# Writing row sums element-interleaved in four groups in a four-layer graph kernel

## What is computed

```
def _layernorm(x, axis=-1, eps=1e-05):
    m = jnp.mean(x, axis=axis, keepdims=True)
    v = jnp.var(x, axis=axis, keepdims=True)
    return (x - m) / jnp.sqrt(v + eps)
...
x = _layernorm(x + _L0_gnn_ref(...))   # attention over edges, softmax per target
x = _layernorm(x + _L1_gnn_ref(...))   # mean of neighbours, two linear maps, relu
x = _layernorm(x + _L2_gnn_ref(...))   # one matrix per edge type (8), sum per target
x = _layernorm(x + _L3_gnn_ref(...))   # relu messages of 3 types, 3 node types, residual
```

## Time and profile before

| | us |
|---|---|
| median of 3 runs | 1827.29 (1821.63 to 1827.8) |
| profiled execution | 1824.94 |
| its span on the core | 1822.8 |
| VectorE busy | 1518.1 (83%) |
| TensorE matmul busy | 1447.3 (79%) |
| ScalarE busy | 1085.2 (60%) |
| GpSimd busy | 1221.6 (67%) |

### The profile page before, as it was taken

One profiled execution on the slowest core, in us unless ns is written; L12 is line 12 of the kernel. 1 busy time (PEld: TensorE's weight loads), 2 busy tenths in 40 slices (PEclk: granted clock), 3 DMA queues, 4 the chain that ended last, 5 costly groups with the idle time before them and its releaser, 6 DMA issues.

```text
span 1822.8 us, 24302 instructions
## 1 busy us (share of the span) xinstructions
PE 1447.3 (79%) x6228; PEld 920.3 (50%) x6228; DVE 1518.1 (83%) x4392; ACT 1085.2 (60%) x2688; POOL 1221.6 (67%) x910
## 2 busy tenths in 40 slices
PE   2677777777787737877888499999898499999995
PEld 1344444444454425666666355555555255555552
DVE  3999999999999947999999589999999366666663
ACT  0467777777777754999999735655555233333331
POOL 7467666666766737888883188877772557777764
PEclk8789989899989878999999789999999799999998
DMA  5334444444444335676675445455442333443320
GB/s 145 84 79 100 100 105 105 93 101 97 96 107 105 62 94 126 180 189 181 187 189 159 126 111 128 124 132 138 130 107 76 100 88 88 98 98 90 88 75 21
DMA packets 165804, 205.15 MB, mean 113 GB/s; under 512 B 66823, under 2 KB 97918, under 8 KB 165666
## 3 DMA queue, kind: packets, MB, share of 16 engines
q1 hardware_dynamic: 108066, 179.45, 37.3%
q0 software_dynamic: 57600, 24.15, 7.5%
HBM read 147.12 MB, written 70.80 MB: 120 GB/s over the span
## 4 chain that ended last, share of the span: by engine, by line
DVE 59%; PE 27%; issue 8%; ACT 3%; DMA 1%; SPq 1%; POOL 0%; DVEq 0%; POOLq 0%; ACTq 0%
PE po L1210 16%; DVE bst L660 16%; DVE masked L866 5%; DVE run L738 5%; DVE po L707 4%; DVE sel L709 4%; DVE y L703 3%; DVE po L706 3%; DVE y L698 2%; PE pt L1195 2%; PE po L1205 2%; PE pb L1433 2%; PE pa L1474 1%; PE pc L1474 1%; PE pb L1474 1%
## 5 line engine op out<-in xcount | busy, mean ns | idle before, releaser
L475 POOL DMA_INDIRECT xs<-target_rows,slot_all x276 | 385.7, 1397 | 235.4 <-DMA xs<-source_rows 156.1
L951 ACT ACTIVATE x<-y,nmr,rst 125x128 f32<-125x128 f32 x800 | 322.7, 481 | 47.5 <-DVE nmr L688 47.5
L1210 PE MATMUL po<-wnt,rt 128*125 128x384 f32 x800 | 311.6, 538 | 0.6 <-ACT rt L988 0.6
L475 POOL DMA_INDIRECT xs<-in_x,src_all x100 | 148.1, 1481 | 136.2 <-issue 136.2
L1210 PEld LDWEIGHTS po<-wnt,rt 128*125 128x125 f32 x800 | 172.9, 216 | 117.0 <-issue 40.2
L1205 PE MATMUL po<-ball,ones_bf 128*125 128x512 bf16 (+1 forms) x512 | 153.2, 429 | 80.5 <-DVE sel L709 76.5
L1195 PE MATMUL pt<-ident,x 125*128 125x125 f32 x800 | 125.1, 280 | 99.5 <-issue 73.1
L1210 PE MATMUL po<-wnt,run 128*125 128x384 f32 x600 | 201.5, 486 | 0.0
L482 POOL DMA_INDIRECT out_rows<-do,last_all x100 | 121.5, 1215 | 89.9 <-ACT do L951 48.4
L660 DVE BATCH_NORM_STATS2 bst<-y 125x6 f32<-125x128 f32 x800 | 164.8, 278 | 3.8
L951 ACT ACTIVATE do<-yd,nmr,rst 125x128 f32<-125x128 f32 x400 | 163.6, 482 | 6.6 <-DVE nmr L688 6.6
(11 more groups left out here) (188 smaller groups left out, 3150.0 us busy)
## 6 DMA issues: line engine op xcount, KB each, us to landing
xin<-in_x SPq DMA_DIRECT2D x100, 224.0 KB
out_rows<-res SPq DMA_DIRECT2D x100, 224.0 KB
same<-same_d SPq DMA_DIRECT2D x75, 250.0 KB, 4.0
source_rows<-so SPq DMA_DIRECT2D x75, 224.0 KB
target_rows<-do SPq DMA_DIRECT2D x75, 224.0 KB
xs<-source_rows SPq DMA_DIRECT2D x69, 224.0 KB
xd<-target_rows SPq DMA_DIRECT2D x59, 224.0 KB
rel<-in_etype SPq DMA_DIRECT2D x50, 250.0 KB, 4.7
```

The lines of the kernel that those rows point to most:

```text
L475: return nc.gpsimd.indirect_dma_start(out=to, out_offset=None, in_=table, in_offset=bass.IndirectOffsetOnAxis(ap=index, axis=0), bounds_ch ...
L951: last = A(to[:, j, :], y[:, j, :], ACT.Identity, scale=rst[s][:, k:k + 1], bias=nmr[s][:, k:k + 1])
L1210: last = mm(po[0:R, j * 512:j * 512 + NT * D], left(j), wnt[:, k, :, :].rearrange("k t d -> k (t d)"), start=False, stop=stop, skip_group_ ...
```

## The change

Every tile of sums that goes to `stats` and `normalize` keeps its 512 places per partition, but element d of row group j is written at place d·4 + j instead of j·128 + d. The new view `woven` does that: its step from one element of a row to the next is four float32, that is 16 bytes.

`stats` then issues one `bn_stats` for two groups j and j + 1. Its input runs over d with the pair inside: 256 elements, two neighbours and then a gap of two. The even places are group j and the odd ones group j + 1, so the six numbers are already the two groups' count, mean and sum of squares, and `bst` shrinks to three numbers for each group. `variances` becomes one `scalar_tensor_tensor` and one `tensor_tensor`, with constants from a small tile `floors`; `scales` takes the mean from `bst`. In layer 0 the product of `yd` goes to a plain scratch tile (`ys[0]`) and only the final sum is written woven. The copy of statistics in layer 1 becomes a `tensor_tensor` max of the values with themselves, 12 elements in place of 24. `normalize` reads its 128 values at the 16-byte step and writes them contiguously as before.

```diff
-        bst = two(sb, "bst", [R, G * T, 6])
-        msum, mdif, ve, seed, rst, nmr, tmp = (two(sb, n, [R, G * T]) for n in ...
+        bst = two(sb, "bst", [R, G * T, 3])
+        floors = sb("floors", [R, 2])
...
+        woven = lambda a: a[:, :, :].rearrange("p j d -> p (j d)").rearrange("p (d j) -> p j d", j=T)
...
             def stats(y, s, g):
-                for j in range(T):
-                    last = V.bn_stats(bst[s][:, g * T + j, :], y[:, j, :])
+                for j in range(0, T, 2):
+                    to = bst[s][:, g * T + j:g * T + j + 2, :].rearrange("p j k -> p (j k)")
+                    last = V.bn_stats(to, woven(y)[:, j:j + 2, :].rearrange("p j d -> p d j"))
                 return last
...
-                V.tensor_tensor(md[:, g], b_[:, g, 1], b_[:, g, 4], ALU.subtract)
-                V.tensor_tensor(ms[:, g], b_[:, g, 1], b_[:, g, 4], ALU.add)
-                step(V.tensor_tensor(v[:, g], b_[:, g, 2], b_[:, g, 5], ALU.add))
-                step(V.scalar_tensor_tensor(out=q[:, g], in0=md[:, g], scalar=D / 4.0, in1=md[:, g], ...))
-                step(V.tensor_tensor(v[:, g], v[:, g], q[:, g], ALU.add))
+                v, m2 = ve[s], bst[s][:, :, 2]
                 if twice:
-                    last = V.tensor_scalar(v[:, 0:both], v[:, 0:both], 1.0 + EPS, D * EPS * EPS, ALU.mult, ALU.add)
+                    last = V.scalar_tensor_tensor(out=v[:, 0:both], in0=m2[:, 0:both], scalar=1.0 + EPS,
+                                                  in1=floors[:, 0:1].broadcast_to([R, both]), op0=ALU.mult, op1=ALU.add)
                 if n > twice:
-                    last = V.tensor_scalar(v[:, both:n * T], v[:, both:n * T], D * EPS, None, ALU.add)
+                    last = V.tensor_tensor(v[:, both:n * T], m2[:, both:n * T],
+                                           floors[:, 1:2].broadcast_to([R, n * T - both]), ALU.add)
...
-                    V.tensor_tensor(y0[d % 4][:, :, :], xin[d % 4][:, :, :], bias_rows, ALU.add).then_inc(s_y0, 1)
+                    V.tensor_tensor(woven(y0[d % 4]), xin[d % 4][:, :, :], bias_rows, ALU.add).then_inc(s_y0, 1)
...
-                V.tensor_tensor(yd[b][:, :, :], yd[b][:, :, :], xd3[c % 3][:, :, :], ALU.add).then_inc(q["nF"], 1)
+                V.tensor_tensor(woven(yd[b]), ys[0][:, :, :], xd3[c % 3][:, :, :], ALU.add).then_inc(q["nF"], 1)
...
-                return V.tensor_copy(bst[s][:, T:2 * T, :], bst[s][:, 4 * T:5 * T, :])
+                edge = bst[s][:, 4 * T:5 * T, :]
+                return V.tensor_tensor(bst[s][:, T:2 * T, :], edge, edge, ALU.max)
...
-                    last = A(to[:, j, :], y[:, j, :], ACT.Identity, scale=rst[s][:, k:k + 1], bias=nmr[s][:, k:k + 1])
+                    last = A(to[:, j, :], woven(y)[:, j, :], ACT.Identity, scale=rst[s][:, k:k + 1], bias=nmr[s][:, k:k + 1])
```

More of the change, by code:

```diff
@@ L124, in gnn_kernel @@
         G = 8
-        bst = two(sb, "bst", [R, G * T, 6])
-        msum, mdif, ve, seed, rst, nmr, tmp = (two(sb, n, [R, G * T]) for n in
-                                                   ("msum", "mdif", "ve", "seed", "rst", "nmr", "tmp"))
+        bst = two(sb, "bst", [R, G * T, 3])
+        floors = sb("floors", [R, 2])
+        ve, seed, rst, nmr, tmp = (two(sb, n, [R, G * T]) for n in ("ve", "seed", "rst", "nmr", "tmp"))
         xs, xd = [sb(f"xs{i}", [R, T, D]) for i in range(3)], two(sb, "xd", [R, T, D])
@@ L604, in _ @@
                 V.memset(bst[k][:, :, :], 0.0)
+            V.memset(floors[:, 0:1], D * EPS * EPS)
+            V.memset(floors[:, 1:2], D * EPS)
             V.memset(carry[:, :], 0.0)
@@ L682, in scales @@
                 g = slice(0, n * T)
-                ms, v, e, r, t, m = (a[s] for a in (msum, ve, seed, rst, tmp, nmr))
+                b_, v, e, r, t, m = (a[s] for a in (bst, ve, seed, rst, tmp, nmr))
                 dve.wait_ge(s_seed, next(seeds))
@@ L702, in read @@
                     dve.wait_ge(s_x3, at(d - 6))
-                    last = V.scalar_tensor_tensor(out=y1[(d - LAG) % 4][:, :, :], in0=of_z, scalar=0.0,
+                    last = V.scalar_tensor_tensor(out=woven(y1[(d - LAG) % 4]), in0=of_z, scalar=0.0,
                                                   in1=x1[(d - LAG) % 4][:, :, :], op0=ALU.max, op1=ALU.add)
@@ L708, in read @@
                     dve.wait_ge(s_out, at(m - 3))
-                    last = V.scalar_tensor_tensor(out=sel[m % 4][:, :, :], in0=x3[m % 4][:, :, :], scalar=2.0, in1=of_type(0),
+                    last = V.scalar_tensor_tensor(out=woven(sel[m % 4]), in0=x3[m % 4][:, :, :], scalar=2.0, in1=of_type(0),
                                                   op0=ALU.mult, op1=ALU.add)
@@ L787, in source_rows0 @@
                 dve.wait_ge(q["nS"], at(c - 1))
-                V.tensor_tensor(ysb[b][:, :, :], xs[k][:, :, :], bias_rows, ALU.add).then_inc(q["yb"], 1)
+                V.tensor_tensor(woven(ysb[b]), xs[k][:, :, :], bias_rows, ALU.add).then_inc(q["yb"], 1)
             scores(0)
@@ L874, in target_rows2 @@
                 dve.wait_ge(q["xd"][b], counted(c, ROWS))
-                step(V.tensor_tensor(yd[b][:, :, :], xd[b][:, :, :], flat_bank(pa), ALU.add))
+                step(V.tensor_tensor(woven(yd[b]), xd[b][:, :, :], flat_bank(pa), ALU.add))
                 return stats(yd[b], s, 3)
@@ L921, in updated_rows @@
                 dve.wait_ge(q["nD"], at(c - 1))
-                V.scalar_tensor_tensor(out=yd[b][:, :, :], in0=xd3[c % 3][:, :, :], scalar=2.0, in1=of_type(0),
+                V.scalar_tensor_tensor(out=woven(yd[b]), in0=xd3[c % 3][:, :, :], scalar=2.0, in1=of_type(0),
                                        op0=ALU.mult, op1=ALU.add).then_inc(q["rd"], 1)
```

12 lines of the change are left out of this document (5 added, 7 removed).

## The result

| | before | after |
|---|---|---|
| median, us | 1824.55 (1821.63 to 1827.8) | 1970.97 (1967.57 to 1972.15) |
| ratio | | 1.0799, interval 1.0771 to 1.0827 |
| span of the profiled execution, us | 1822.8 | 1969.2 |

The change makes the kernel 8% slower. The sign was forecast; the size was not: the time lies above the 1918 us of the forecast and above the 1950 us at which its range ends.

A forecast was written before the change was run, and what follows sets the result against it. VectorE was taken to bound layers 0 and 2, with ScalarE just behind in layer 1, and TensorE layer 3. Layers +29, +50, +6, +5 and dense chunks +3 gave +93 on 1824.9: 1918 us; forecast's own range 1880 to 1950, 8-in-10 range 1725 to 1950.

The forecast's parts named there:

- Gain 1, statistics: One bn_stats over 256 elements takes 0.34 us, saving 0.86, 0.54 and 0.43 us per chunk in layers 0, 1, 2.
- Gain 2, variances: Two small VectorE operations replace seven, 0.20 us staying; saves 0.91, 1.1 and 0.79 us per chunk in layers 0, 1, 2.
- Cost 1, writes: VectorE's writes at a 16-byte step cost 0.71 ns more per element, 0.36 us per tile, the upper bound.
- Cost 2, reads: Each ScalarE ACTIVATE reading at a 16-byte step grows by 0.128 us, on top of its fixed part.
- The sum, layer 0: VectorE gets +1.15 us per chunk; ScalarE's 21.9 us stay under VectorE's 25.9; +29 us in all.
- Layer 1: ScalarE becomes the bound with 14.8 us per chunk, +50 us in all; about 1945 us if its waits aren't absorbed.
- Layer 3: Woven sum L922 grows 0.36 us, 0.17 us covered before TensorE starts; 0.2 us come through, +5 us in all.
- The passages between layers: Dense chunks alone, six blocks: ACTIVATEs 1.5 us more, VectorE about 1 less, +0.5 us each, +3 us.
- A: Rival: both 16-byte steps, VectorE's writes and ScalarE's reads, are free; 1728 us, chance 0.28.
- B: Rival: ScalarE's strided reads pay and VectorE's strided writes don't; 1811 us, chance 0.14.
- C: Rival: VectorE's strided writes pay and ScalarE's strided reads don't; 1870 us, chance 0.05.
- D: Rival: 256-element bn_stats runs at the strided price, about 1.4 us more per layer 0 chunk, +70 us; chance 0.03.

The follow-up runs named there:

- the run with writes alone: The changed kernel with ScalarE's normalizing reads plain again, VectorE still writing woven: 1866.69 us, ratio 1.0213 to the kernel before.
- the gains alone: The changed kernel with plain writes and plain ScalarE reads, keeping only pair statistics and short variances: 1756.00 us, ratio 0.9618 to before.
- the reads alone: The changed kernel with all VectorE sums written contiguously, ScalarE still reading woven: 1928.93 us, ratio 1.0558 to the kernel before.
- the alternate rows: The changed kernel with nothing woven; bn_stats takes 256 elements alternately from two plain rows 512 bytes apart: 1759.99 us, ratio 0.9635 to before.

## Why the prediction was right or wrong

**Gain 1, statistics: right.** The 256-element instruction takes 410 ns where one of 128 took 278 on average; four in a row take 1.41 us in after's timeline, (1.41 − 0.41)/3 = 0.33 us from start to start against the 0.34 worked out. The value chosen between the bounds was the right one.

**Gain 2, variances: right.** 0.18 us stay of 1.11, against 0.20. (Of the seven small operations three stand in a `step`, not five.)

**Cost 1, writes: right in price.** 0.80 ns per element at L704 and 0.75 at L710 (1069 − 687 ns) against 0.71. Taking the upper bound from the nearest row held, though for a reason that the row alone did not give (above). In layer 2 the writes cost 13.02 to 14.44, 1.42 us against 1.45 in the sum.

**Cost 2, reads: right in price, 0.123 us against 0.128,** and right in that the stream comes on top of the fixed part. By the Trainium skill, "ScalarE: Activation LUTs", What ACT_TABLE_LOAD costs, the time of an ACTIVATE is a fixed part, one for each pointer operand and one per element. It says nothing of steps; that a slower stream is added and not hidden is what this trace shows, 604 ns for the woven against 482 for the plain read.

**The sum, layer 0: wrong, 27 of the 53 us that are missing.** The step that failed is "21.9, still under VectorE's 25.9": ScalarE's busy time was compared with a period, as if the engines ran side by side. ScalarE's 21.7 us came true, but 5.6 us of waits for TensorE stand between its instructions, and the chunk took 27.29 us. The idle 6.7 us of ScalarE before, which looked like cover, were mostly such waits (6.0 us). What the forecast had no term for is the ring of hand-overs from VectorE over TensorE and ScalarE back to VectorE: it had 0.55 us of slack before, and the woven sums (1.5 us), TensorE's lower clock (1.4 us) and the longer reads (0.6 us) on it closed it. VectorE's +1.15 us per chunk are right by themselves (25.95 us in the run with writes alone, 25.9 forecast).

**Layer 1: right in mechanism, 9 us short.** ScalarE became the bound: 283.12 of 300 us busy, 14.6 us of the 15.5, against 14.8. The waits in its queue were left out again, although the prediction named them as its upper case. VectorE now waits 2.58 us for seeds, which follow ScalarE's eight ACTIVATEs for `so` and `so3`. VectorE's row, then ScalarE's:

```profile
906.04 0.18 DVE L686 SCALAR_TENSOR_TENSOR tmp<-seed 125x24 f32<-125x24 f32 x1 [2.58 <-ACT seed L962]
```

```profile
901.48 4.16 ACT L953 ACTIVATE so<-ys,nmr,rst 125x128 f32<-125x128 f32 x8
905.54 0.21 ACT L960 ACTIVATE seed<-ve 125x24 f32<-125x24 f32 x1
```

**Layer 2: right,** +3.9 against +6.

**Layer 3: half the size.** 0.17 us between the end of L922 and TensorE's start were taken for cover. They were not: 0.38 of the 0.40 us by which the sum grew came through. After, TensorE waits, and nearly the same 0.15 us stand there; the sum ends at 1747.71 and TensorE starts at 1747.86; VectorE's row, then TensorE's:

```profile
1746.62 1.09 DVE L924 SCALAR_TENSOR_TENSOR yd<-xd,po 125x512 f32<-125x512 f32 x1
```

```profile
1746.64 1.00 PE L1476 MATMUL pc<-st,wet 128*128 128x500 f32 x2
1747.86 0.83 PE L1207 MATMUL po<-ball,ones_bf 128*125 128x384 bf16 x4 [0.21 <-DVE yd L924]
```

From the last pair of message products to the bias products it was 0.84 us and is 1.22, 0.38 us more: nearly the whole price of one woven sum, 25 times, 9.5 us.

**The passages between layers: wrong, 15 us.** Here the last chunks of a layer run with little beside them, and the +3 us for dense chunks alone were a guess. The passages grew by 6.7, 8.7 and 2.7 us. Which engine's work they are was not taken apart.

**The rivals.** A, both steps free, is excluded by the durations; its time, 1728 us, was too low even for the kernel that has the gains alone (1756), by 28 us. There layer 0 reached 23.62 and not 22.9, with waits of 0.5 us each for seeds and z products. B's case, the reads alone, came out 118 us above its figure (1929 against 1811), by the same failed step. C's case, the writes alone, came out at 1867 against 1870. D, statistics at the strided price, did not happen; its sum doesn't follow from its own price either: sixteen instructions at 0.18 us more each are 2.9 us per chunk in layer 0, not 1.4.

The Trainium skill, "SBUF — State Buffer", Specifications (TRN2), wants two uses of a 16-byte line for full bandwidth. The durations agree: steps of 16 bytes cost 0.8 ns per element on VectorE, steps of 8 bytes nothing there. The same row of the Trainium skill's table says that each crossing to a new line costs something; for the alternate rows that comes to 5 ns in 256 crossings (415 against 410 ns). The Trainium skill's free stride of "4 fp32" (same page, Door 1: The DMA port swizzle) does not hold for either engine if it is read as a step of four.

## What to carry to other kernels

A step of four float32 in SBUF costs 0.75 to 0.8 ns per element on VectorE's writes and 0.12 us on a 128-element ACTIVATE; a step of two is free, and so is an instruction that takes its elements in turn from two contiguous rows. So one `bn_stats` can serve two rows without any change of layout. Before work is added to an engine with idle time, look at what its waits are. If they are hand-overs, follow the chain from engine to engine round one period, and see how much slack it has: here ScalarE's 6.7 us of idle time were 0.55 us of slack in the chunk shown, and work on any engine of the chain counted once that was used up.

## What the runs showed of the hardware

- VectorE: a 512-element sum with a plain output 0.69 us, with an output step of 16 bytes 1.07 to 1.09 us, of 8 bytes 0.68 us.
- ScalarE: a 128-element ACTIVATE with two pointer operands 0.482 us plain, 0.490 us at 8 bytes, 0.604 us at 16 bytes.
- `bn_stats` over 256 elements takes 0.41 us in all and 0.33 us from start to start, whether the pairs are neighbours or lie 512 bytes apart; one over 128 takes 0.28 us in all and 0.20 us from start to start.
- VectorE to TensorE by a semaphore: in layer 3 0.15 to 0.17 us from the end of the one to the start of the other, in layer 0 0.05 us (`sel` ends at 518.87, TensorE starts at 518.92).
- In layer 1 before, a 24-element copy and the small scalings of the variances took up to 0.42 and 0.66 us (the earlier trace rows has the copy with 0.40 us), while the two-input forms that replace them take 0.17 us. What holds the former was not tested.
